# A decoder layer whose cross attention carries side work: other seats for it, queries read by VectorE, keys and values projected once

## The reference

```python
x = layernorm(x + attention(x))                      # 16 heads of 64, rotary, causal
x = layernorm(x + deformable_cross_attention(x, ctx))
x = layernorm(x + gated_ffn(x))                      # fake-quantised, inner width 704

# the cross attention, per sequence: ctx has 77 rows, 16 heads of 16, 5 samples a query
K, V = ctx @ Wk.T + bk, ctx @ Wv.T + bv
Qp   = x @ Wq.T + bq
off  = Qp @ Woff.T + boff                            # 16 heads x 5 offsets
loc  = mod(ref + off + token, length - 1)
i0, dx = floor(ix(loc)), ix(loc) - floor(ix(loc))
sk = 0.5 * ((1 - dx) * K[i0] + dx * K[i0 + 1])       # rows outside 0..76 count as zero
sv = 0.5 * ((1 - dx) * V[i0] + dx * V[i0 + 1])
out = (softmax(Qp / 4 . sk) over the 5 samples) . sv @ Wo.T + bo
```

## Time and profile before

| | us |
|---|---|
| median of 3 runs | 2012.91 |
| lowest, highest | 2007.72, 2015.58 |
| the profiled execution, its own time | 2010.13 |
| its span, first to last instruction | 2008.4 |
| cross attention in it: first value copy to last | 1350.38 to 1851.34 |

### The profile page before, as it was taken

How to read it: one execution, slowest core, us unless ns; L and a number is a source line. 1 busy time by engine, 2 the same in 40 slices (tenths; PEclk the granted TensorE clock), 3 DMA queues, 4 the chain that set the end, 5 groups by cost and what they waited for, 6 DMA issues and landing times. The chain is left out here.

```text
span 2008.4 us, 43270 instructions
## 1 busy us (share of the span) xinstructions
PE 1813.4 (90%) x17210; PEld 1104.9 (55%) x17210; DVE 1514.5 (75%) x2149; ACT 1321.1 (66%) x1803; POOL 1485.8 (74%) x1113
## 2 busy tenths in 40 slices
PE   5989999999999999999999999999989999897475
PEld 3545545455545554555555545557768777675233
DVE  6757868779678777787886876846777777778687
ACT  3546666656566566566665666758897878986387
POOL 0668869778778697696877877656898899849357
PEclk8989999999999999999999999999999999998698
DMA  7122042031131320322212205000000000000002
GB/s 219 47 53 69 17 106 69 17 80 47 44 80 27 85 70 17 86 53 54 70 28 74 69 17 163 12 24 13 14 3 9 2 3 3 3 3 2 2 1 84
DMA packets 57736, 92.39 MB, mean 46 GB/s; under 512 B 25536, under 2 KB 35776, under 8 KB 53568
## 3 DMA queue, kind: packets, MB, share of 16 engines
q1 hardware_dynamic: 48608, 89.37, 17.1%
q10 hardware_dynamic: 8928, 0.26, 0.2%
HBM read 51.33 MB, written 4.46 MB: 28 GB/s over the span
## 5 line engine op out<-in xcount | busy, mean ns | idle before, releaser
L1391 POOL TENSOR_TENSOR acc<-acc,probs 128x768 f32<-128x768 f32 (+1 forms) x316 | 578.8, 1832 | 112.5 <-ACT probs L883 82.4
L883 ACT ACTIVATE probs<-psum 128x1024 f32<-128x1024 f32 (+3 forms) x384 | 290.6, 811 | 160.4 <-PE psum L613 160.4
L827 ACT ACTIVATE chunks<-psum 128x1024 bf16<-128x1024 f32 x288 | 282.2, 1026 | 130.4 <-PE psum L572 83.4
L2076 ACT ACTIVATE onehot<-psum 128x1024 bf16<-128x1024 f32 x315 | 324.0, 1058 | 1.3 <-PE psum L1906 1.1
L605 PE MATMUL psum<-operands 64*128 64x512 f32 (+3 forms) x1536 | 305.9, 509 | 18.0 <-ACT chunks L827 17.2
L1105 DVE TENSOR_REDUCE lows<-chunks 128x2 f32<-128x1024 bf16 (+1 forms) x224 | 266.9, 1218 | 71.5 <-ACT chunks L827 61.6
L1925 PE MATMUL psum<-pieces,onehot 128*128 128x64 bf16 x7680 | 274.6, 195 | 14.6 <-DVE prod L2227 14.2
L1925 PEld LDWEIGHTS psum<-pieces,onehot 128*128 128x128 bf16 x7680 | 257.3, 99 | 45.6 <-issue 20.7
L1370 POOL TENSOR_SCALAR_AFFINE_SELECT probs<-probs 128x256 f32<-128x256 f32 x256 | 152.8, 614 | 134.6 <-ACT probs L883 134.4
L1039 DVE SCALAR_TENSOR_TENSOR turned<-staged,bqk,rot 128x512 f32<-128x512 f32 x128 | 157.8, 1272 | 64.4 <-ACT staged L865 64.4
L605 PEld LDWEIGHTS psum<-operands 64*128 64x128 f32 x1536 | 128.9, 185 | 136.3 <-issue 62.7
(11 more groups left out here) (277 smaller groups left out, 3538.1 us busy)
## 6 DMA issues: line engine op xcount, KB each, us to landing
operands<-turned SPq DMA_DIRECT2D x124, 256.0 KB, 5.0
rden<-inverse_rows SPq DMA_DIRECT2D x64, 256.0 KB, 3.9
raw<-in_wqk SPq DMA_DIRECT2D x30, 256.0 KB, 4.5
y<-in_x SPq DMA_DIRECT2D x1, 4096.0 KB, 17.5
wo<-in_wo SPq DMA_DIRECT2D x16, 256.0 KB, 2.6
out<-res SPq DMA_DIRECT2D x16, 256.0 KB, 2.1
raw<-in_wv SPq DMA_DIRECT2D x15, 256.0 KB, 4.6
raw<-in_xT SPq DMA_DIRECT2D x12, 256.0 KB, 4.1
```

The lines of the kernel that those rows point to most:

```text
L827: nc.scalar.activation(chunks[k % MBUF][:, :, :], slot("max", n, c)[:, :, :], ACT.Copy, scale=-1.0)\
L883: nc.scalar.activation(probs[u % PBUF][:, :, 0:width], slot("s", n, u)[:, :, 0:width], ACT.Exp, scale=1.0 / D ** 0.5).then_inc(s_exp, 1)
L1391: G.tensor_tensor(dst, dst, src, ALU.add).then_inc(s_acc, 1)
L2076: A.activation(onehot[n % 2][:, k, :], bc[m % 2], ACT.Relu).then_inc(s_oh, 1)
```

## The change

All seats but those of `x1T`, `off` and `i0` are moved. `cT` riders 0 to 3 now ride in heads 12 and 13 of their own batch and 4 to 7 in units (4, 2) to (5, 1) of the next; `out` and `q` get one seat in every second unit; `kv` has two riders for four. DVE reads the `q` riders, adding the bias on the way (`bias_q` on DVE), in place of a copy on ACT and four additions on POOL. The context is projected once, DVE writes two of the four rows of `kvd`, and SP moves them one partition down by a transfer from `kvd` to `kvd` (127 partitions of 2 x 256 floats), for which POOL's split waits (`s_shift`). Row 0 of the moved ones is set to zero once. `kvd` is laid as (4, 256), so POOL reads it in runs of 16 when it makes the pieces. In the opening `open_kv` is two multiplications of 512 columns, and the same transfer is issued by SP ahead of the load of `wo`.

```diff
-RIDERS = {"x1T": KT * TILE_PAIRS, "off": TILE_PAIRS, "kv": 4, "q": TT, "i0": NHP // 2, "cT": KT * TILE_PAIRS,
+RIDERS = {"x1T": KT * TILE_PAIRS, "off": TILE_PAIRS, "kv": 2, "q": TT, "i0": NHP // 2, "cT": KT * TILE_PAIRS,
           "out": TT}
 RIDERS_AT = {"x1T": [(0, 0), (0, 1), (0, 2), (0, 3), (1, 0), (1, 1), (1, 2), (1, 3)],
              "off": [(2, 0), (2, 2), (3, 0), (3, 2)],
-             "kv": [(5, 0), (5, 2), (6, 0), (6, 2)],
-             "q": [(9, 0), (9, 2), (10, 0), (10, 1), (10, 2), (11, 0), (11, 1), (11, 2)],
-             "i0": [(14, 0), (14, 1), (14, 2), (15, 0)],
-             "cT": [(2, 1), (2, 3), (3, 1), (3, 3), (4, 0), (4, 1), (4, 2), (4, 3)],
-             "out": [(5, 1), (5, 3), (6, 1), (6, 3), (7, 0), (7, 2), (8, 0), (8, 2)]}
+             "kv": [(2, 1), (3, 1)],
+             "cT": [(12, 1), (12, 3), (13, 1), (13, 3), (4, 2), (4, 3), (5, 0), (5, 1)],
+             "out": [(5, 2), (6, 0), (6, 2), (7, 0), (7, 2), (8, 0), (8, 2), (9, 0)],
+             "q": [(9, 2), (10, 0), (10, 2), (11, 0), (11, 2), (12, 0), (12, 2), (13, 0)],
+             "i0": [(14, 0), (14, 1), (14, 2), (15, 0)]}
-LATE_RIDERS_AT = {(13, 1): ("cT", 0), (13, 3): ("cT", 1), (14, 1): ("cT", 2), (14, 3): ("cT", 3)}
-X2_STATISTICS_AT = [(7, 1), (9, 2)]
+X2_STATISTICS_AT = [(7, 1), (9, 1)]
 def rider_at(b, h, u):
-    if b == LATE and (h, u) in LATE_RIDERS_AT:
-        kind, i = LATE_RIDERS_AT[h, u]
-        return kind, b, i
     kind, i = RIDER_AT.get((h, u), (None, 0))
     if kind == "out":
         return kind, b - 1, i
+    if kind == "cT" and i < TILE_PAIRS:
+        return kind, b, i
     if kind == "cT":
         return (kind, b - 1, i) if b else None
...
-                elif kind == "q":
-                    act.wait_ge(s_qd, count(kind, b, i))
-                    A.activation(q[b % 2][:, i, :].rearrange("p (h n) -> p h n", n=P), seat(kind, b, i), ACT.Copy)\
-                     .then_inc(s_qc, 1)
...
+            def bias_q(b, t):
+                dve.wait_ge(s_qd, count("q", b, t))
+                V.tensor_tensor(q[b % 2][:, t, :].rearrange("p (a n) -> p a n", a=2), seat("q", b, t),
+                                bq.rearrange("p (a n) -> p a n", a=2), ALU.add).then_inc(s_qb, 1)
...
-            def bias_q(b):
-                pool.wait_ge(s_qc, RIDERS["q"] * b)
-                tiles = TT // BIAS_PARTS
-                for part in range(BIAS_PARTS):
-                    rows_q = q[b % 2][:, tiles * part:tiles * (part + 1), :]
-                    G.tensor_tensor(rows_q, rows_q, bq.unsqueeze(1).broadcast_to([P, tiles, E]), ALU.add).then_inc(s_qb, 1)
...
             def scale_kv(b, i):
-                v, s = divmod(i, 2)
                 dve.wait_ge(s_kv, count("kv", b, i))
                 if i == 0:
                     dve.wait_ge(s_pieces, b)
-                V.scalar_tensor_tensor(out=kvd[:, :, 2 * s + v, :].rearrange("p (a h) d -> p a h d", a=2),
-                                       in0=seat("kv", b, i).rearrange("p a (h d) -> p a h d", d=HD),
-                                       scalar=kv_scale[:, v, s:s + 1],
-                                       in1=kv_bias[:, v, s, :].rearrange("p (a h d) -> p a h d", a=2, d=HD),
+                V.scalar_tensor_tensor(out=kvd[:, 2 * i + 1, :].rearrange("p (a e) -> p a e", a=2), in0=seat("kv", b, i),
+                                       scalar=kv_scale[:, i:i + 1], in1=kv_bias[:, i, :].rearrange("p (a e) -> p a e", a=2),
                                        op0=ALU.mult, op1=ALU.add).then_inc(s_kvr, 1)
...
-            for b in range(1, XB - 1):
-                sp.wait_ge(s_kv, RIDERS["kv"] * (b + 1))
-                sp.wait_ge(s_len, b + 1)
-                load_context(b + 1)
+            for b in range(1, XB):
+                sp.wait_ge(s_kvr, RIDERS["kv"] * (b + 1))
+                sp.dma_start(kvd[1:P, 0:4:2, :], kvd[0:P - 1, 1:4:2, :]).then_inc(s_shift, 16)
+                if b == 1:
+                    sp.wait_ge(s_wo, RIDERS["out"])
+                    sp.dma_start(wo[:, :, :], dram["xwo"]).then_inc(s_xwo, 16)
+                if b + 1 < XB:
+                    sp.wait_ge(s_kv, RIDERS["kv"] * (b + 1))
+                    sp.wait_ge(s_len, b + 1)
+                    load_context(b + 1)
...
             def split_kv(b):
-                pool.wait_ge(s_kvr, RIDERS["kv"] * (b + 1))
+                pool.wait_ge(s_shift, 16 * (b + 1))
...
             def open_kv(dst):
                 pe.wait_ge(s_in, 16 * 2)
-                for v in range(2):
-                    for s in range(2):
-                        for kt in range(KT):
-                            last = nc.tensor.matmul(dst[:, v, s * E:(s + 1) * E], opening.ctxT[:, v, kt, :],
-                                                    opening.wkv[:, kt, s * E:(s + 1) * E],
-                                                    start=kt == 0, stop=kt == KT - 1)
+                for kt in range(KT):
+                    last = nc.tensor.matmul(dst[:, 0, :], opening.ctxT[:, kt, :], opening.wkv[:, kt, :],
+                                            start=kt == 0, stop=kt == KT - 1)
```

More of the change, by code:

```diff
@@ L469, in _ @@
                     spread_inverses(n - 1)
+                if i == GROUPS - 1:
+                    sp.wait_ge(s_kvr, RIDERS["kv"])
+                    sp.wait_ge(s_set, 10)
+                    sp.dma_start(opening.kvd[1:P, 0:4:2, :], opening.kvd[0:P - 1, 1:4:2, :]).then_inc(s_shift, 16)
                 splits = splits_of(i) if i + 2 < GROUPS else []
@@ L962, in copy_piece @@
                 act.wait_ge(s_whq, 2)
-                nc.scalar.activation(opening.pieces[:, p, :, :, :], opening.kvd[:, :, :, :], ACT.Copy)\
+                nc.scalar.activation(opening.pieces[:, p, :, :, :],
+                                     opening.kvd[:, :, :].rearrange("p c (h d) -> p h c d", d=HD), ACT.Copy)\
                   .then_inc(s_diff if p < PIECES - 1 else s_pieces, 1)
@@ L1208, in open_scales @@
                 dve.wait_ge(s_oconst, 16 * 9)
-                for v in range(2):
-                    for s in range(2):
-                        first.done(V.tensor_scalar(opening.kv_scale[:, v, s:s + 1], opening.valid[:, v:v + 1],
-                                                   0.5 if s else 0.5 * HD ** -0.5, None, ALU.mult))
+                for s in range(2):
+                    first.done(V.tensor_scalar(opening.kv_scale[:, s:s + 1], opening.valid, 0.5 if s else 0.5 * HD ** -0.5,
+                                               None, ALU.mult))
                 first.settle()
-                for v in range(2):
-                    for s in range(2):
-                        first.done(V.tensor_scalar(opening.kv_bias[:, v, s, :], opening.bkv[:, s * E:(s + 1) * E],
-                                                   opening.kv_scale[:, v, s:s + 1], None, ALU.mult))
+                for s in range(2):
+                    first.done(V.tensor_scalar(opening.kv_bias[:, s, :], opening.bkv[:, s * E:(s + 1) * E],
+                                               opening.kv_scale[:, s:s + 1], None, ALU.mult))
                 first.done(V.tensor_tensor(opening.table[:, :, :], opening.ref.unsqueeze(1).broadcast_to([P, TT, HK]),
@@ L1241, in open_read @@
                     dve.wait_ge(s_s, NU * (PAIRS - 2))
-                    for v in range(2):
-                        for s in range(2):
-                            V.scalar_tensor_tensor(out=opening.kvd[:, :, 2 * s + v, :],
-                                                   in0=src[:, v, s * E:(s + 1) * E].rearrange("p (h d) -> p h d", d=HD),
-                                                   scalar=opening.kv_scale[:, v, s:s + 1],
-                                                   in1=opening.kv_bias[:, v, s, :].rearrange("p (h d) -> p h d", d=HD),
-                                                   op0=ALU.mult, op1=ALU.add).then_inc(s_kvr, 1)
+                    for s in range(2):
+                        V.scalar_tensor_tensor(out=opening.kvd[:, 2 * s + 1, :], in0=src[:, 0, s * E:(s + 1) * E],
+                                               scalar=opening.kv_scale[:, s:s + 1], in1=opening.kv_bias[:, s, :],
+                                               op0=ALU.mult, op1=ALU.add).then_inc(s_kvr, 1)
                 elif name[0] == "q":
@@ L1451, in _ @@
                         G.memset(opening.i0b[:, :, :, :], 1.0).then_inc(s_set, 1)
+                        G.memset(opening.kvd[0:1, 0:4:2, :], 0.0).then_inc(s_set, 1)
                     if (n, m) in REST_AT:
@@ L1886, in wait_slot @@
                     elif kind == "q":
-                        pe.wait_ge(s_qc, RIDERS["q"] * (b - 1) + i + 1)
+                        pe.wait_ge(s_qb, count(kind, b, i))
                     elif kind == "i0":
@@ L1945, in project_kv @@
                 for half in range(2):
-                    c = s * E + half * P
+                    c = i * E + half * P
                     for kt in range(KT):
```

(11 more changed lines are left out.)

73 lines of the change are left out of this document (32 added, 41 removed).

## The result

| | before | changed |
|---|---|---|
| median of the runs (4 each) | 2012.46 us | 1995.47 us (1994.64 to 1996.86) |
| ratio | | 0.9912, 95% interval 0.9896 to 0.9928 |
| median, measured again (13 and 6 runs) | 2009.41 us | 1993.64 us |
| ratio there | | 0.9924, 0.9905 to 0.9943 |
| span of the profiled execution | 2008.4 us | 1995.1 us; second trace 1991.3 us |

The change makes the kernel 0.8 to 0.9% faster, 16 to 17 us. The forecast was 22 us less, 1990. The changed kernel was profiled twice; its second execution is called the second trace here.

The account below looks back on a forecast made before the run. PE, busy 90% of the span, was taken to set the time. Batches -20.2 and opening -1.8 gave -22.0 us: 1988.1 from 2010.1, with the median 2.8 above, forecast 1990 us; range for 8 in 10, 1979 to 2003.

Parts of the forecast that it names:

- The seats: Moved riders in cross attention: -2.9, -6.9, -6.9 and -3.5 us in batches 0 to 3, together -20.2 us.
- Heads 7, 8 and 9 stay.: Cross attention, worked for batch 1: these three heads keep their length, no gain or loss counted.
- what would prove it wrong: Listed signs: PE waiting for a gather at head 12, softmax steps of 1 us in new heads, DVE last in heads 9-13.
- Head 4: Batch 1: from 11.59 to 8.2 us, -3.4, bounds 6.5 and 8.6; batch 3: from 10.78 to 7.5, -3.2.
- the stop: PE's 3.43 us wait at head 4's first `cT` transpose for DVE's last gather of the round before; claimed to go.
- Who reads the queries: DVE reads eight `q` riders a batch, +2.5 us of DVE, costed at nothing as covered by PE; POOL loses 5.2 us.
- The softmax of head 12: Three DVE steps of 2.7 us together become 1.0 without POOL's query additions: 1.7 us saved, in three batches 5 us.
- The shifted keys and values: Transfer within SBUF lands after 5.0 us, covered by 15 us of heads 4 and 5: costs nothing, else up to 5 us a batch.
- The opening: Four PE instructions of 512 columns take at most half of 3.7 us: -1.8 us, bounds 0 and -2.5.
- The stop did not move to (12, 1): Rival: PE's wait for the gather reappears at head 12's first `cT` transposes, 18 us in four batches, 2008 us; chance 0.08.
- DVE holds: Rival: DVE's new reads cost heads 3, 4 and 9 to 13 0.5 us more each, 10 us in three batches, 2000; chance 0.15.
- POOL is not the bound: Denies the rival that POOL, busy 109.4 us per batch, becomes the bound and the kernel gets slower by 10 us; chance 0.03.

Follow-up runs that it names:

- The split cut in two: Changed kernel with POOL's split of keys and values in two parts, two tensor_scalar locate parts between: 1989.91 us, ratio 0.9903; again 1991.12 us, 0.9889.
- the idle additions: Changed kernel plus four unused tensor_tensor additions on POOL, where the kernel before added to the queries: 2000.3 us, ratio 0.9951.

## Why the prediction was right, and where its size was off

The direction, its main causes and the range held; the forecast was 5.5 us low. (Its own sum, 1988.1 + 2.8, gives 1990.9 and was written as 1990.) In the batches, where the forecast has 480.8 us, the second trace has 483.9.

- **The seats.** Right. With the cover of the transfer that they bring they are worth 10 to 13 us. Of batch 1, heads 5, 6 and 13 came out at 6.95, 7.43 and 7.31 (forecast 7.1, 7.5, 7.2), heads 10 and 11 at 7.55 and 7.44 (7.6), heads 2 and 3 at 8.07 and 8.34 (8.3 and 8.2), head 12 at 8.23 (8.6). The prices of a rider and of a transpose held.
- **"Heads 7, 8 and 9 stay."** This is the step that failed. Head 8 grew by 1.8 us in batches 0 and 1 and by 0.6 in batch 2, 4.2 in all. The prediction had listed the mechanism under what would prove it wrong (softmax steps of 1 us or more in new heads, as POOL's work shifts against DVE's), but gave it no price. The split cut in two took back 3.4 us of the 4.2 and the idle additions made such a loss anew in head 12, so the cause is shown. That it came from the heads ahead being shorter is read from the timelines and was not tried by itself.
- **Head 4** was mis-sized: 9.0 us in batches 1 and 2 against 8.2, outside the bounds of 6.5 and 8.6. PE's timeline there:

```profile
1502.60 1.03 PE L1923 MATMUL psum<-pieces,onehot 128*128 128x64 bf16 x30 [1.14 <-DVE prod L2222]
...
1506.16 0.41 PE L1987 MATMUL psum<-xident,ctx 128*128 128x128 f32 x2 [0.91 <-DVE prod L2222]
...
1509.80 0.39 PE L1904 MATMUL psum<-i0T,near 32*128 32x512 bf16 x2 [0.46 <-ACT onehot L2073]
```

  The head without waits is 9.00 - 2.51 = 6.49 us, the forecast's 6.5, and the stop, the clock and the transposes went as it said. But the waits, taken as 1.7 us, are 1.14 + 0.91 + 0.46 = 2.5 (the last is for ACT's one-hot): DVE is late before the sample of (4, 0) too, and the working counted only what follows it. That is 0.8 us in two batches. In batch 3 the forecast was 7.5; the head took 8.1 where its clock was 1.00 (five runs with the change's seats), and 8.9 and 9.35 at 0.82 in the changed kernel.
- **Head 6 of batch 2** took 8.63 us in both traces where 7.5 was forecast, which nothing in the forecast covers. DVE has a reduction of 2.3 us in (5, 1) of that batch alone, and PE waits for the product behind it:

```profile
1640.67 2.27 DVE L2179 TENSOR_REDUCE y_top<-y 128x1 f32<-128x2048 f32 x1
```

```profile
1644.22 1.02 PE L2000 MATMUL psum<-wo,ctxT 128*128 128x128 f32 x7 [1.15 <-DVE prod L2222]
```

  Before, heads 5 and 6 held four float32 riders in front of and behind it, and head 6 of batch 2 was as long as in the other batches (9.35). So this is head 8 once more: work of another engine that heavy heads had covered shows when they get lighter. No run moved it.
- **The granted clock.** Of the changed kernel's 487.7 us, 3.7 are in stretches that the second trace ran faster: head 0 of batch 0 (5.96 against 5.03), head 9 of batch 1 (8.99 against 7.44) and heads 4 and 5 of batch 3 (17.5 against 16.3). Batch 3 at 118.07 against the forecast's 115 owes part of its excess to it; in five of the runs with the change's seats it was 115.4 to 116.3. Seven traces have the whole split under the softmax of head 8 as the changed kernel has it. In head 9 of batch 1 six of them have a clock of 0.81 to 0.83, in head 9 of batch 0, behind the same 2.6 us of idle PE, none has. What decides whether such a stretch is granted the full clock is not known from these runs.
- **Who reads the queries.** At nothing, as forecast: with heads 10 to 12 bound by PE, DVE's reads are covered. Given back to ACT and POOL, with the new seats, it costs 7 to 9 us, a coupling between the parts that the sum of terms had not seen. For the same reason this and the price of the seats do not add up to the gain.
- **The softmax of head 12.** The forecast took 1.7 us off for POOL's additions, and the idle additions cost 1.82, so the term is right. But its sign, three steps near 0.32 us, did not come: the first takes 1.51 under POOL's last locate part. It cost nothing, as head 12 is bound by PE; that was luck.
- **The shifted keys and values.** Covered, as forecast, but by luck of the margin. The estimate of 5.0 us to landing was wrong by a factor of three (14.7 us), and the cover was larger than the 15 us assumed: issued at 1498.40, wanted at 1530.65, 32 us. In the old seats, where it was issued later, it was not covered. In the opening it did show, at a place where it costs PE nothing:

```profile
1301.96 1.62 POOL L1411 TENSOR_TENSOR kvd<-kvd 128x512 f32<-128x512 f32 x1 [3.62 <-DMA kvd<-kvd]
```

- **The opening.** PE's four instructions take 1.98 us against 3.7, a little over half and not at most half, so PE has 1.7 us less to do. That the launch got shorter by it no run shows: the traces of both kernels have the same 1507.4 us outside the four batches, and those of all runs scatter there from 1505.7 to 1511.3. The term of 1.8 stands as not shown.

```profile
1283.15 1.98 PE L698 MATMUL psum<-xwkv,xctxT 128*128 128x512 f32 x4
```

- **The rivals.** The stop did not move to (12, 1): PE is busy 8.23 of the 8.23 us of head 12. DVE holds heads 4 and 8: head 8 by its slow steps, which are no new reads; in head 4 no run parts what makes it late, but the head of batch 0 has 7.15 us before and after, with the new `kv` read ahead of it. POOL is not the bound: it waits for DVE's weights as before, only its order matters.

The Trainium skill, page "SBUF — State Buffer", section "Who interferes with whom", states that a VectorE instruction with two SBUF inputs and a GpSimd instruction that reads SBUF lock each other out for a whole instruction. The traces agree for POOL's tensor_tensor and cast, to 0.18 us. For its tensor_scalars over 128x640 they agree for the beginning alone, and here the prediction read the earlier trace rows too far: the step of 0.33 us there began 0.98 us behind the start of POOL's instruction (1544.37 against 1543.39). Over all traces the 30 steps that began within 0.4 us of the start of a tensor_scalar of 1.8 or 2.4 us were held, and ended 0.89 to 0.98 us behind that start; the 134 that began 0.62 us or more behind it took 0.31 to 0.33 us, as if nothing ran beside them. So such an instruction holds a step too, but only in its first 0.9 to 1.0 us, and there the measurement decides against "whole".

## What to carry to other kernels

Where one engine's steps are locked out by another's, a change that shortens the stretch between them moves the meeting point: look up, for every head whose neighbours change, what the other engine will issue beside its short steps, and give that a price even where the head itself is left alone. A cheap remedy is the other engine's order: put the instructions that do least harm where the short steps come. And a slow step costs only where the bound engine has no work of its own left: 1.2 us vanished in head 12 for nothing, while 1.85 us past that point cost 1.82.
